# Attention with a condition: the condition's load in larger pieces, the first weights issued by ScalarE, shorter zero products

## What is computed

```python
Q = _split_heads(x @ Wq.T + bq)          # x: (8, 512, 512), 16 heads of 32
K = _split_heads(x @ Wk.T + bk)
V = _split_heads(x @ Wv.T + bv)
cQ = Q + _split_heads(tokens @ Wq.T + bq)   # tokens = cond[:, None, :], cond: (8, 512)
cK = K + _split_heads(tokens @ Wk.T + bk)
scores = jnp.einsum('bhqd,bhkd->bhqk', cQ, cK) / jnp.sqrt(jnp.float32(HEAD_DIM))
attn = jax.nn.softmax(scores, axis=-1)
out = jnp.einsum('bhqk,bhkd->bhqd', attn, V)
x = x + out                              # heads merged again
```

## Time and profile before

| | |
|---|---|
| median of 3 runs | 661.04 us (660.73 to 662.91) |
| the profiled execution's own time | 662.08 us |
| its span, first to last instruction | 660.3 us |
| PE busy | 652.3 us, 99% |
| DVE, ACT, POOL busy | 82%, 57%, 74% |

### The profile page before, as it was taken

How to read it: one execution, slowest core, us unless ns; L and a number is a source line. 1 busy time by engine, 2 the same in 40 slices (tenths; PEclk the granted TensorE clock), 3 DMA queues, 4 the chain that set the end, 5 groups by cost and what they waited for, 6 DMA issues and landing times.

```text
span 660.3 us, 10095 instructions
## 1 busy us (share of the span) xinstructions
PE 652.3 (99%) x3556; PEld 444.4 (67%) x3556; DVE 540.8 (82%) x819; ACT 373.4 (57%) x659; POOL 485.9 (74%) x202
## 2 busy tenths in 40 slices
PE   8999999999999999999999999999999999999997
PEld 5776776666776666776666776666776666676442
DVE  4586888888888888888888888888888888887887
ACT  6335565555665555665555665555655555555673
POOL 5519677789777789777779777779777778766890
PEclk9999999999999999999999999999999999999999
DMA  8934335554334554334554434554334544336401
GB/s 289 222 87 101 92 91 132 144 145 111 107 95 123 145 144 114 107 99 117 145 145 118 109 98 113 143 146 122 105 102 107 145 129 113 82 93 150 130 18 64
DMA packets 48278, 79.87 MB, mean 121 GB/s; under 512 B 9826, under 2 KB 9826, under 8 KB 48226
## 3 DMA queue, kind: packets, MB, share of 16 engines
q1 hardware_dynamic: 47700, 79.21, 44.5%
q10 hardware_dynamic: 528, 0.02, 0.0%
HBM read 19.95 MB, written 8.39 MB: 43 GB/s over the span
## 4 chain that ended last, share of the span: by engine, by line
PE 93%; DVE 4%; DMA 1%; SPq 1%; ACT 0%; issue 0%
PE bank L291 26%; PE bank L395 19%; PE bank L415 17%; PE bank L374 17%; PE bank L351 13%; DVE mf L700 3%; DMA Pt<-xT 1%; PE bank L446 1%; SPq L960 0%; PE bank L324 0%; DMA Qs<-mt 0%; PE bank L423 0%; PE bank L336 0%; SPq L935 0%; DVE bank L700 0%
## 5 line engine op out<-in xcount | busy, mean ns | idle before, releaser
L610 ACT ACTIVATE Pt<-bank 128x512 f32<-128x512 f32 x512 | 299.6, 600 | 227.7 <-PE bank L395 156.0
L700 DVE TENSOR_REDUCE mf<-bank 128x1 f32<-128x512 f32 x496 | 333.4, 686 | 73.6 <-PE bank L374 70.6
L887 POOL TENSOR_TENSOR A<-A,Pt 128x2048 f32<-128x2048 f32 x59 | 270.8, 4589 | 4.6
L395 PE MATMUL bank<-Qs,Ks 98*128 98x512 f32 x496 | 199.0, 403 | 0.6 <-ACT Pt L610 0.5
L374 PE MATMUL bank<-Ks,Qs 96*128 96x512 f32 x496 | 198.1, 399 | 0.4 <-DVE mf L700 0.3
L887 POOL TENSOR_TENSOR A<-Pt 128x2048 f32<-128x2048 f32 x30 | 138.4, 4612 | 2.8 <-DVE part_sums L725 2.0
L395 PEld LDWEIGHTS bank<-Qs,Ks 98*128 98x128 f32 x496 | 93.3, 188 | 50.9 <-ACT Pt L610 27.5
L415 PE MATMUL bank<-Pt,V 128*32 128x512 f32 x1024 | 119.1, 596 | 0.1
L857 POOL TENSOR_TENSOR Xl<-xr,Xh 128x512 fp32r<-128x512 f32 x28 | 36.1, 1289 | 112.7 <-ACT Xh L573 112.7
L374 PEld LDWEIGHTS bank<-Ks,Qs 96*128 96x128 f32 x496 | 93.8, 189 | 27.7 <-DVE mf L700 5.0
L291 PE MATMUL bank<-Xh,Wh 128*128 128x512 f32 x256 | 102.3, 400 | 0.8 <-ACT Xh L565 0.8
(11 more groups left out here) (70 smaller groups left out, 374.7 us busy)
## 6 DMA issues: line engine op xcount, KB each, us to landing
Qs<-hi SPq DMA_DIRECT2D x60, 256.0 KB, 3.6
Ks<-hi SPq DMA_DIRECT2D x60, 256.0 KB, 3.6
Qs<-lo SPq DMA_DIRECT2D x30, 256.0 KB, 4.1
Ks<-lo SPq DMA_DIRECT2D x30, 256.0 KB, 3.2
xr<-xT SPq DMA_DIRECT2D x28, 256.0 KB, 2.7
res<-xT SPq DMA_DIRECT2D x28, 256.0 KB, 2.9
outT<-ot SPq DMA_DIRECT2D x28, 256.0 KB, 3.2
Qs<-mt SPq DMA_DIRECT2D x124, 4.0 KB
```

What stands on the lines that cost most here:

```text
L395: e.matmul(st_bank(u)[:, :], k[0:98, j, kc * P:(kc + 1) * P], q[0:98, j, :], start=True, stop=True).then_inc(t_st, 1)
L610: e.activation(exponentials(g)[:, kc, j, :], st_bank(u)[:, :], ACT.Exp, scale=SCALE).then_inc(a_e, 1)
L700: e.reduce_max(to[:, 4 * j + qc:4 * j + qc + 1], MXB[u % 2][:, :], AXX).then_inc(v_mx, 1)
L887: e.tensor_tensor(sums, ex[:, 0, :, :] if kc == 1 else sums, ex[:, kc, :, :], ALU.add).then_inc(p_a, 1)
```

## The change

The condition goes to a tile `cond` of its own: each partition's 4x8 values are one piece of 128 bytes (128 pieces in all), where the load into `cT` had one piece of 32 bytes for each partition and chunk (512). ScalarE no longer waits before it issues this load, and then issues the load of q's first weights, which SyncE issued before. VectorE copies `cond` into the zero-filled `cT`. The zero products become 3 of 256 columns and 1 of 64, all ahead of the condition's product. One more projection matmul stands before the first maximum, and `MORE_AT` moves from 22 to 23, so that the total is the same.

```diff
-WARM, WARM_MORE, V_AHEAD, MORE_AT = 4, 2, 7, 22
+WARM, WARM_MORE, V_AHEAD, MORE_AT = 3, 1, 8, 23
...
+        cond = sb("cond", [P, KC, B])
...
                 for i in range(WARM):
                     e.matmul(MXB[0][:, 0:256], res[:, 0:P], res[:, 0:256], start=True, stop=True)
-
-            def warm_up_more():
                 for i in range(WARM_MORE):
                     e.matmul(MXB[0][:, 0:64], res[:, 0:P], res[:, 0:64], start=True, stop=True)
...
                 if qk == 0 and i == 0:
-                    e.wait_ge(d_c, 16)
+                    e.wait_ge(v_c, 4)
...
             condition(0, 0)
-            warm_up_more()
...
-            e.wait_ge(v_c, 1)
-            e.dma_start(cT[:, :, 0:B], condT).then_inc(d_c, 16)
+            e.dma_start(cond[:, :, :], condT).then_inc(d_c, 16)
+            e.dma_start(wraw[0][:, 0, :], wdram[0][0]).then_inc(d_w[0][0], 16)
...
+            e.wait_ge(v_c, 1)
+            e.wait_ge(d_c, 16)
+            e.tensor_copy(cT[:, :, 0:B], cond[:, :, :]).then_inc(v_c, 1)
             x0_lo(0)
...
-            load_x0(0)
-            w(0, 0)
-            for kc in range(1, KC):
+            for kc in range(KC):
                 load_x0(kc)
```

## The result

| | before | changed |
|---|---|---|
| median | 660.95 us (21 runs, 660.21 to 663.18) | 662.58 us (21 runs, 661.46 to 663.28) |
| ratio | | 1.002, 95% interval 1.0013 to 1.0026 |
| span of the profiled execution | 660.3 us | 660.8 us |
| its own time | 662.08 us | 662.59 us |

The account below looks back on a forecast made before the run. TensorE is busy 99% of the span, so only an earlier start of its unbroken stream counts. From cases of 0 to +0.15 and 0 to -0.3 us it set -0.35 against the median: 660.7 us, range 659.6 to 661.9.

Parts of the forecast that it names:

- the first gate: First projection on TensorE, needing q's first rounded weights: could begin at about 5.2 instead of 5.83, 0.6 us earlier.
- the loads: Opening DMA loads: first x chunk up to 0.3 us later, weights no later than 4.5; 0 to 0.1 us lost.
- a clock that rises later: Rival: TensorE's fast clock comes later in the opening, giving 661.8 to 662.8 us; 18% together with other losses.
- The earlier issue of the chunks: x chunks 1 to 3 issued 0.46 us earlier: gain taken as 0, since transfers, not issues, set the pace.
- The first gate's lead: Of the projection's 0.6 us earlier start, 0.15 to 0.2 us remain, since VectorE's rests limit the following matmuls.
- The sum: Against the profiled execution: 0 to +0.15 us with the fourth chunk late again, 0 to -0.3 with it in time.
- The condition's transfers: Condition's load in a quarter of the pieces: all loads behind it gain about 0.1, at most 0.14 us.
- The second gate: TensorE's 1.01 us idle for the late fourth x chunk: moves 0.1 us if late again, vanishes in both kernels otherwise.
- The third gate: First maximum, waiting for Ks: only 0.55 us winnable; the matmul moved ahead costs 0.24 us, free if Ks is awaited.

Follow-up runs that it names:

- e3: Changed kernel with q's first weights issued by SyncE again, behind x chunk 0; ratio to the kernel before 1.0010.
- e14: The changed kernel itself, unaltered, measured and profiled a third time; ratio to the kernel before 1.0011.
- e4: Kernel before with one more projection matmul ahead of the first maximum (8 and 23 for 7 and 22), nothing else; ratio 1.0012.
- e9: Kernel before with the new condition load and VectorE's copy, GpSimd's fills of Ks held until that copy is done; ratio 1.0002.
- e12: Kernel before with new condition load, GpSimd's fills held, weights by SyncE, 4 zero products of 256 columns and none of 64, 7 and 22; ratio 1.0002.
- e8: Changed kernel with longer zeros, 4 products of 256 columns and 1 of 64, all ahead of the condition's product; ratio to the kernel before 1.0005.
- e15: Changed kernel with 4 zero products of 256 columns and 1 of 64, plus one more small load on SyncE; ratio to the kernel before 1.0002.
- e16: Changed kernel with zeros 4 and 1, one more small SyncE load, 7 and 22, GpSimd's fills held until the copy; ratio to the kernel before 1.0000.
- e5: The changed kernel itself, unaltered, measured and profiled a second time; ratio to the kernel before 1.0017.
- e7: Kernel before with only the new condition load in 128 pieces, issued without a wait, and VectorE's copy; ratio 1.0008.

## Why the prediction was wrong

**The step that failed** is in the first gate and the loads: "it may land up to 0.3 us later, and the weights no later than 4.5", and on it "the condition's product waits for the weights at about 4.5 anyway". The first chunk did land in time (3.6); the weights landed at 5.1. I gave the sharing of the DMA engines to x chunk 0, which was nearly through, and none of it to the weights, which had x chunk 1 beside them. The prediction's own pace gives the landing: two loads at 0.75 us each, side by side from 3.55 on, both end at about 5.05 (an estimate from its rows). The Trainium skill (DMA: Bandwidth & Descriptors, section "Queues, rings and completion order") says that each DMA engine goes round between its queues packet by packet; the landings at 5.1 and 4.9 agree.

**What followed from it** was in the text as a rival: a clock that rises later, at 661.8 to 662.8; the median came at 662.58. I gave that case and all other losses 18%, since I set its condition at idle time "from 5.0 to 5.2". With the weights at 5.1 the pause was 0.5 to 0.7 us and came before the clock was up. Its price was near: nine matmuls at 0.2 us more are 1.8 us, and the traces of one program give 1.8 to 1.95. In the profiled execution nine ran slow.

**The earlier issue of the chunks** was put at nothing, and that was wrong too, without harm. In the ten traces with ScalarE's weights the fourth chunk is issued at 2.14 and lands at 6.3 to 7.0; in the seven others beside the profile of before it is issued at 2.61 and lands at 6.9 to 7.7. It is under way for 4.5 us in the mean of the ones and 4.7 of the others, so it lands about 0.6 us earlier, 0.47 of it by its issue. The Trainium skill (DMA: Bandwidth & Descriptors, section "Issuing engines are not separate DMA queues") was cited in the prediction for a term of 0; but it says that the sequencer's time is saved, and this time is what came out. TensorE gained next to nothing by it: of the seventeen traces only e3 shows a wait behind that chunk, 0.18 us.

**The first gate's lead** of 0.15 to 0.2 us never came, not even with the clock in time. e14 began the projection 0.17 us before the kernel before (5.66 for 5.83), but `Wl`, made from the late weights, was ready at 5.64 + 0.69 = 6.33 for 5.85, and the eighth and ninth matmul started at 7.79 and 8.02 for 7.54 and 7.78: 0.24 us behind. Its first maximum at 22.50 is 1.3 us ahead of the kernel before's profile all the same, since that profile took 1.44 us longer from the ninth to the twelfth matmul (7.78 to 10.13, for 8.02 to 8.93 in e14), where its late fourth chunk stands.

**The sum** had a slip besides: "-0.2 to -0.4" with +0.24 where the DMA is no gate, and without it where it is one, gives 0 to -0.4 and not 0 to -0.3; and the -0.35 of the forecast was set and not worked out.

**The condition's transfers**: landed sooner as forecast (at 3.6 to 4.1 us, for 4.5 to 5.9 before), which removes a pause that the kernel before has in some executions. But its copy was costed at nothing with the cover of ScalarE's 4.27, and at under 0.69 us without it. It has a third neighbour, GpSimd: 0.29 to 0.57 us where it ends with the first fill, which was covered, and 1.90 us where it ends with the second.

**The second gate**: the fourth chunk was late in the profile of before alone (8.4 us); in the other traces it landed between 6.3 and 7.8. Its lateness is seen in 1 of 18 executions, as the prediction left open, and it made the profile of before look worse than the kernel is.

**The third gate**: `V_AHEAD` as forecast, 0.38 to 0.42 us at the first scores matmul with 8, 0.16 to 0.20 with 7, in all eighteen traces. The gate at `Ks` is real as well: it landed between 21.8 and 24.3, and TensorE waited for it in e4, e9 and e12. There a gain in the opening is given back. For the versions that did not wait there (e8, e15 and e16, first maximum at 22.5 to 22.9) it is not shown what keeps them level with the kernel before; one candidate is that an ordinary execution of that kernel has no late chunk, as its median, 1.1 us under its profiled execution, suggests.

**Not foreseen** was SyncE's late start, 0.3 us at 608 us: the prediction said that all edits act before 45 us.

**The split of the loss**: 0.8 us by the clock (e8 against e5), 0.2 us by the moved matmul and 0.3 us by SyncE (from their waits), together 1.3 us; the three ratios of the changed kernel say 0.7 to 1.3 us. The clock's share is an average over executions with and without slow matmuls, and the agreement is loose: the timed part is known to some 0.6 us, and only the two small ones come from traces. Open is what makes SyncE late once at a fixed place of its program (only that the place moves with one DMA is shown), why e4's median is 0.5 us off although its trace has 0.2, and what makes a second wait for `Ks` near 51 us, 0.2 to 0.7 us in thirteen traces, come and go.

## What to carry to other kernels

A load that is moved to another issuing queue gains its issue time and loses its place in line: look at what is issued beside it at that moment, and let both end when the two would have ended one after the other. Zeros that warm TensorE should last until the work that follows is there in its latest execution, not in the profiled one; here the pause between them cost more than the zeros did. And an effect of 1 us in a kernel whose executions differ by 2 us is read from several traces of one program, since one of them may hold a late load or a late clock that the others don't.

## What the runs showed of the hardware

- Six to ten of TensorE's first projection matmuls ran at the slow level in 7 of 10 traces with a pause of 0.46 to 1.33 us in its first 6 us, and none to three in the 8 without. One program gave 0, 9 and 10 slow matmuls, and its first maximum at 22.50, 24.30 and 24.45 us. A projection matmul of 128x512 takes 0.63 us at the slow level and 0.40 at the fast one, a weight load of 128x128 0.33 and 0.19. The granted clock of the profile reads 1.00 in all of these stretches.
- VectorE's copy of 128x32 float32 takes 0.18 us with no fill beside it (e9, e12, e16) and up to 1.90 us beside a GpSimd fill of 2x2048, which takes 1.80; it ends with the fill. VectorE's subtraction of 128x512 takes 0.69 us beside the fill or not, unless it stands behind such a copy (1.49 us in e7).
- A load of 16 KB in 512 pieces of 32 bytes was under way for 3.4 to 4.8 us in four executions; in 128 pieces of 128 bytes, and issued 0.3 us earlier, for 2.9 to 3.3 in fourteen.
- A load of 256 KB took 3.0 to 3.3 us where SyncE issued it between two others, and 3.7 to 4.1 where ScalarE issued it at the same moment as SyncE its next load.
- SyncE starts one group of DMAs 0.33 us later than its others, at a place of its program that moved from 272 to 608 us when one DMA was taken out ahead of it, and back when one was put in.
